# A decoder layer on one core: three plain feed-forward chunks instead of four, with the row sums packed three pairs to a chunk

## What is computed

```python
x = _layernorm(x + _L0_attn_ref(x, Wqkv, bqkv, Wo, bo))        # self attention
x = _layernorm(x + _L0_xattn_ref(x, ctx_4096, Wq, bq, Wk, bk)) # attention to 375 context rows
# the feed-forward part, with weights of 4 bits (INTER = 2752)
Wg, Wu, Wd = _dequant(gate...), _dequant(up...), _dequant(down...)
h = jax.nn.silu(xf @ Wg) * (xf @ Wu)
x = _layernorm(x + h @ Wd)
```

## Time and profile before

| | |
|---|---|
| median of the runs | 1820.59 us (1817.97 to 1821.37, 3 runs) |
| the profiled execution | 1816.36 us, its span 1814.6 us |
| TensorE busy, of the span | 1729.8 us (95%) |
| mean granted clock of TensorE | 0.991 of full speed |
| VectorE, ScalarE, GpSimd busy | 1106.1, 494.1, 500.2 us |
| plain chunks 1 to 3 on TensorE | about 701 to 820 us of the span |
| mixed chunks 4 to 20 | from 821.5 us |

### The profile page before, as it was taken

The page is one execution under the profiler, slowest core; times in us unless marked ns, Lnnn a source line. Parts: engine busy times, 40 slices in busy tenths (PEclk is TensorE's granted clock), DMA queues, the critical chain, the costliest instruction groups (busy, mean ns, idle before and its releaser), DMA issues.

```text
span 1814.6 us, 26677 instructions
## 1 busy us (share of the span) xinstructions
PE 1729.8 (95%) x9784; PEld 976.8 (54%) x9784; DVE 1106.1 (61%) x1656; ACT 494.1 (27%) x734; POOL 500.2 (28%) x326
## 2 busy tenths in 40 slices
PE   5999999898999989999999999999999899999998
PEld 3677644686878744444444444444445344444443
DVE  7787578676888877666777777877874111111111
ACT  3323110544655543322233232332332000000000
POOL 0333388133333326542232232232231000000000
PEclk8999999999999999999999999999999999999999
DMA  9353433899999967762213223223124812222120
GB/s 327 108 155 119 148 119 86 166 218 243 239 231 248 233 139 182 176 130 67 70 48 90 55 48 97 49 51 94 49 60 124 321 55 109 82 81 108 54 108 23
DMA packets 335590, 231.89 MB, mean 128 GB/s; under 512 B 288224, under 2 KB 302624, under 8 KB 333348
## 3 DMA queue, kind: packets, MB, share of 16 engines
q1 hardware_dynamic: 329284, 227.85, 48.1%
q10 hardware_dynamic: 6240, 3.15, 0.6%
HBM read 122.93 MB, written 60.83 MB: 101 GB/s over the span
## 4 chain that ended last, share of the span: by engine, by line
PE 53%; issue 25%; DVE 10%; SPq 5%; DMA 4%; ACT 1%; POOL 1%; DVEq 0%; POOLq 0%; ACTq 0%
PE psum L1671 51%; SPq L2201 4%; DMA arena<-arena 3%; DVE arena L814 1%; DVE arena L490 1%; PE psum L1922 1%; PE psum L1848 1%; DVE arena L1024 1%; DVE arena L1022 1%; DVE arena L1019 1%; PE psum L1684 1%; DVE arena L879 1%; DMA arena<-in_L_attn_Wqkv 1%; DVE arena L997 1%; POOL small L1180 1%
## 5 line engine op out<-in xcount | busy, mean ns | idle before, releaser
L1671 PE MATMUL psum<-arena 128*128 128x448 f16 (+6 forms) x7176 | 1266.9, 337 | 34.5 <-DMA arena<-arena 21.9
L1671 PEld LDWEIGHTS psum<-arena 128*128 128x128 f16 (+3 forms) x7176 | 750.3, 108 | 531.6 <-issue 85.5
L2025 PE MATMUL psum<-arena 128*128 128x512 f16 x1820 | 393.5, 379 | 6.0 <-DMA arena<-down_weights_scratch 3.7
L2025 PEld LDWEIGHTS psum<-arena 128*128 128x128 f16 x1820 | 177.7, 98 | 221.8 <-DMA arena<-down_weights_scratch 5.4
L1263 POOL TENSOR_TENSOR arena<-arena 128x1024 f16<-128x1024 f32 (+1 forms) x60 | 149.8, 2508 | 415.9 <-ACT arena L1474 415.9
L1162 DVE SCALAR_TENSOR_TENSOR arena<-psum,small,arena 128x512 f32<-128x512 f32 x28 | 20.9, 751 | 331.5 <-PE psum L2025 331.5
L1180 POOL TENSOR_TENSOR small<-small 112x1 f32<-112x1 f32 (+1 forms) x46 | 50.0, 1087 | 489.4 <-DVE small L471 489.4
L1565 ACT ACTIVATE arena<-arena,small 128x448 f32<-128x448 f32 x68 | 45.5, 668 | 207.5 <-DVE arena L1094 144.0
L1474 ACT ACTIVATE arena<-arena 128x1024 f16<-128x1024 f32 (+1 forms) x60 | 68.8, 1173 | 117.9 <-DVE arena L856 89.6
L1254 POOL TENSOR_TENSOR arena<-arena 128x224 f16<-128x224 f32 x64 | 54.3, 848 | 122.1 <-ACT arena L1445 122.0
L854 DVE TENSOR_TENSOR arena<-arena,psum 128x1024 f32<-128x1024 uint32 x65 | 79.1, 1218 | 3.0 <-PE psum L1848 0.9
(11 more groups left out here) (214 smaller groups left out, 1244.6 us busy)
## 6 DMA issues: line engine op xcount, KB each, us to landing
h_scratch<-arena SPq DMA_DIRECT2D x84, 224.0 KB, 2.9
arena<-h_scratch SPq DMA_DIRECT2D x13, 1376.0 KB, 6.1
arena<-in_ctx SPq DMA_DIRECT2D x32, 512.0 KB, 5.1
arena<-in_x SPq DMA_DIRECT2D x32, 448.0 KB, 5.7
x_scratch<-arena SPq DMA_DIRECT2D x32, 448.0 KB, 3.6
arena<-x_scratch SPq DMA_DIRECT2D x32, 448.0 KB, 4.6
arena<-in_L_ffn_down_qweight SPq DMA_DIRECT2D x21, 512.0 KB
down_weights_scratch<-arena SPq DMA_DIRECT2D x20, 512.0 KB, 3.8
```

Source lines behind the costliest of these rows:

```text
L1671: mm = pe.matmul(out, a, r, start=(k == 0), stop=(k == len(pairs) - 1))
L2025: mm = pe.matmul(bk[2 * s + c], ht[s][:, i, a, :], weights_of(i, w, c), start=(i == 0 and (w, a) == PASSES[0]), stop=(i == NI - 1 and (w, ...
```

## The change

`NP` becomes 3: chunks 0, 1 and 2 are plain, and chunk 3 has seven products. Since the loop of mixed chunks takes two chunks per turn and its slots are even and odd chunks, chunk 3 is written out once ahead of the loop on all five engines, and the loop begins with chunk 4 as before. `pair` places three pairs in a chunk: chunk 0 has pairs 0, 1, 2 in places 0, 1, 2, chunk 1 has 3, 4, 5, and chunk 2 has 6 and 7 in places 0 and 1. The mixed chunk that follows the sums is now an odd one, which writes `wgu[1]` in full, so `xabp[0]` moves to the upper part of `wgu[0]`.

```diff
-    NP = 4
+    NP = 3
...
         wgu[0] = carve(at_f, [4 * OPS, 2, P], F16)
+
+        at_spare = at_f + 8 * D
         at_f += OPS * 8 * P * 2
...
         wgu[1] = carve(at_f, [4 * OPS, 2, P], F16)
-
-        at_spare = at_f + 8 * D
         at_f += OPS * 8 * P * 2
...
         def pair(i, k):
-            return [2 * i + k] if i < NP and k < 2 else []
+            return [3 * i + k] if i < NP and 3 * i + k < NPAIR else []
...
             for i in range(NP):
                 chunk(i, i % 2, i // 2, True)
-            with dve.Fori(NP // 2, NI // 2 - 1) as e:
+            mixed_chunk(NP, NP % 2, NP // 2)
+            with dve.Fori((NP + 1) // 2, NI // 2 - 1) as e:
                 for s in range(2):
                     mixed_chunk(2 * e + s, s, e)
```

More of the change, by code:

```diff
@@ L1359, in _ @@
                 chunk(i, i % 2, True)
-            with pool.Fori(NP // 2, NI // 2 - 1) as e:
+            mixed_chunk(NP, NP % 2)
+            with pool.Fori((NP + 1) // 2, NI // 2 - 1) as e:
                 for s in range(2):
@@ L1644, in _ @@
                 chunk(i, i % 2, True)
-            with act.Fori(NP // 2, NI // 2 - 1) as e:
+            mixed_chunk(NP, NP % 2, NP // 2)
+            with act.Fori((NP + 1) // 2, NI // 2 - 1) as e:
                 for s in range(2):
@@ L2005, in _ @@
                 pe.wait_ge(s_tt[i], TT0 + 4 * NB)
-            with pe.Fori(NP // 2, NI // 2 - 1) as e:
+            mixed_chunk(NP, NP % 2, NP // 2)
+            with pe.Fori((NP + 1) // 2, NI // 2 - 1) as e:
                 for s in range(2):
@@ L2395, in _ @@
                 chunk(i, i % 2, P, P)
-            with sp.Fori(NP // 2, NI // 2 - 2) as e:
+            mixed_chunk(NP, NP % 2, P)
+            with sp.Fori((NP + 1) // 2, NI // 2 - 2) as e:
                 for s in range(2):
```

## The result

The changed kernel takes **1833.6 us** (median of 4 runs, 1833.52 to 1835.64) against 1821.0 us (4 runs, 1817.97 to 1822.68): the ratio is 1.0065, with a 95% interval of 1.0044 to 1.0086. It is slower, by 12.6 us, where 5.7 were forecast; the measured time lies 1.1 us above the upper end of the range.

A forecast was written before the change was run, and what follows sets the result against it. TensorE, busy for 95% of the span, was taken to bound the kernel. Terms -4.4 + 7.5 + 1.5 + 1.1 = +5.7 us on a median of 1820.6 gave 1826.3 us, range 1822.0 to 1832.5.

The forecast's parts named there:

- Chunk 3 with seven products, -4.4 us: Chunk 3 drops 24 matmuls on TensorE's path, its period going from 37.83 to 33.42 us: -4.4 us.
- The stall in chunk 1, +7.5: TensorE's second product group of chunk 1 waits for L868 of hidden(0, 3), now behind pair 2: +7.5 us, bounds 6.1 to 11.3.
- the sentence on the GPSIMD Engine Reference of the Trainium skill, section Specifications: Pair 2's row sums in chunk 0: with VectorE idle beside them, L1333 takes 1.53 us not 1.78, 0.25 us lower.
- the 3.1 us estimated from DMA: Bandwidth & Descriptors of the Trainium skill: Pair 2's 448 KB load: 3.1 us from issue, giving a 5.6 us stall; the trace's 5.0 us was used instead.
- The clock, +1.5: TensorE's clock falls to 1.2 GHz after the chunk 1 stall: +1.5 us, between 0 and 3.
- The third pair in chunk 1 and SyncE, +1.1: Later SyncE work delays pair 7, so the wait at chunk 2's gather grows from 3.9 to 5.0 us: +1.1 us.
- the 3.3 us of slack: Chunk 2's second group: L868 of hidden(1, 3) ends 3.3 us before TensorE needs it, so no stall.
- rival 2: TensorE stalls a second time, at chunk 2's second group, as chunk 1's third pair is late: +10.2, 1830.8 us; chance 0.15.
- two slow L1030 (0 to 4 us): Bounds of the +1.1 us at chunk 2's gather: 0 if the load's slack holds, 4 with two L1030 at 4.2 us.
- rival 4: The wait and slow clock (5.4 us) at the last plain chunk's gather vanish through VectorE's and GpSimd's lead: 1819.8 us; chance 0.05.
- The wait at chunk 2's gather: TensorE's wait for the weight sums in the last plain chunk, expected at 4 to 6 us in the new profile.
- the 11.3 us stall: Upper bound of the chunk 1 stall, with the longest load landing (5.8 us) and L1030's longest (4.2 us).

The follow-up runs named there:

- experiment 7: Changed kernel with five plain chunks (NP = 5), pairs two to a chunk in the first four: 1819.5 us, ratio 0.9997 to the kernel before.
- experiment 1: Changed kernel with the third pair's halves (sum_hi, sum_lo) behind hidden(i, 3) instead of ahead of it: 1832.6 us, ratio 1.0058 to the kernel before.
- experiment 5: Changed kernel with the next pair's load ahead of the gate and up DMAs, and a pair's two tiles loaded under two semaphores: 1824.6 us, ratio 1.0013.
- experiment 3: Changed kernel with SyncE issuing the next pair's load ahead of the chunk's gate and up loads: 1827.9 us, ratio 1.0025 to the kernel before.

## Why the prediction was right or wrong

**Chunk 3 with seven products, -4.4 us: right.** The gathers of chunks 3 and 4 stand 33.43 us apart; experiment 7 measures the same worth from the other side.

**The stall in chunk 1, +7.5: right in place, cause and releaser, a little small.** It was 8.22 us, released by L868 behind L1030, L1575 and L1334 (the lines called L1573 and L1333 before the change). The steps that were short are two. The last instruction of the row sums took 2.36 us and not 1.78: VectorE was not idle beside it, as sum_lo of the pair itself (L1030) ran from 719.20 to 720.62. And the second L1030, from 723.11, took 2.03 us and not 1.21: VectorE had nothing else to do, but GpSimd had (L1271, the low part of the down weights that moved behind the pair, 721.94 to 724.06). In both cases the one that began later took longer, by nearly the time that the other still ran: 0.83 us of 1.0, and 0.82 of 0.95. Over the stage L1334 took 2.36 to 2.39 us for the four pairs from pair 1 on where L1030 had begun ahead of it, and 1.53 to 1.55 us for the three where it had not.

That also settles the sentence on the GPSIMD Engine Reference of the Trainium skill, section Specifications: the rule was applied the wrong way round. What it says of VectorE instructions with two SBUF inputs agrees with the 2.36 us: where 0.25 us were taken off by it, 0.58 were to be put on. The load itself landed 4.7 us after its second issue, not in the 3.1 us estimated from DMA: Bandwidth & Descriptors of the Trainium skill; the row was the better guide.

**The clock, +1.5: mis-sized.** Behind the first stall it was 11.97 - 9.25 = 2.7 us. A fall was seen each time that TensorE had idled for 3.9 us or more, but its price lies between 1.5 and 2.7 us and does not follow the length of the wait: 1.6 behind 4.55 us (experiment 1), 2.6 behind 4.06 us and 1.5 behind 4.41 us (experiment 5), 1.8 behind 5.70 us (experiment 3).

**The third pair in chunk 1 and SyncE, +1.1: this step failed.** It was +6.4 us. The forecast followed the pairs through the right links, but gave each the time it had had with two pairs to a chunk. Counted from chunk 0's gather, which came 6.7 us later, store_h was to come at 727.1 and came at 729.30: the transposes (L2317) took 3.2 us each, and the first could only go out behind load_pair(3), which waits for the row sums to end. Pair 4's row sums were to begin at 740.4 and began at 743.63, with a landing of 6.0 us in place of 5.0; pair 5's at 752.1, and began at 755.93; L868 of hidden(1, 3) was to end at 761.0, and ended at 766.4, 5.4 us late. TensorE was itself 2.0 us later than forecast there, so this used up the 3.3 us of slack to the last tenth (its group started at 766.49, 0.15 us late). 2.0 us of the 5.4 are one slow instruction, which rival 2 had named as the danger: the first L1030 of pair 5 took 4.54 us beside GpSimd's L1334 and L1271, and the second, whose high part was ready at 762.63, began at 764.63.

```profile
760.16 5.68 DVE L1030 SCALAR_TENSOR_TENSOR arena<-arena 112x1024 f16<-112x1024 f32 x2 [2.07 <-ACT arena L1575]
```

Then SyncE had to issue the two transposes of pair 5 (1.54 and 3.65 us, from 764.73) before store_h, at 770.07, 13.2 us into chunk 2 and not 7.8. The load of pair 7 landed 26.5 us into chunk 2 instead of 22.1, and 5.9 us later than in the old chunk 3 its row sums began; the last 0.5 us are the sums' own.

What the working lacked was the sum over the loop. Three turns, two of some 12 us inside a chunk and one of 15 to 16 across the next chunk's start, took 39.7 us (pair 1 to pair 4) and 39.8 us (pair 4 to pair 7), more than the 37.8 us of a plain chunk, so any slack given to one pair is used by the next. Bounding this term by two slow L1030 (0 to 4 us) looked at one instruction's spread, which came (4.54 us) and cost 2.0 us; the bound should have been the period of the loop against the time that the chunks leave.

**The forecast as a whole** had the right sign, and its two stalls, no second stall in chunk 2 (rival 2) and no lead that saves the handover (rival 4) are what the trace shows. Of its 5.7 us against 13.3 in the stage, 5.3 are missing at chunk 2's gather, 2.1 at chunk 1's stall and clock, 0.2 behind. The wait at chunk 2's gather, forecast at 4 to 6 us, was 10.19. One sum of the prediction does not come out: the high end of the range is called rival 2 with the 11.3 us stall, which is 10.2 + 3.8 = 14.0, or 1834.6 us, and not 1832.5.

## What to carry to other kernels

Before packing side work closer under a busy engine, take the period of its own loop (load, work, buffer free, next load) and set it against the time each turn is given; work that fits in total can still miss its turn. Look for the chunk where the last turn is wanted early (here the handover, with its wait of 3.93 us) and take work out of that one, instead of spreading it evenly or packing it in front. And when a wait is moved by reordering, follow the engine behind it to its next delivery: experiment 1 moved a stall of 8 us by one gather and gained nothing.

## What had not been expected of the hardware

A DMA transpose kept SyncE busy longer where other transfers were under way: 2.4 to 3.7 us for 13 of the changed kernel's 16 (L2317, median 3.15), against a median of 2.29 and a least of 1.48 us before; the last two, with no load in front of them, took 1.5 us each, and one of pair 5's, 3.2 us behind the issue of a load, 1.54. Loads of the same 448 KB landed between 3.7 and 6.2 us after their issue in this stage. Whether the load itself or the general traffic stretches a transpose was not told apart.
